# A graph network with an expert layer on one core: the stage behind the second aggregation on a ring, with weights and normalised x split into halves beforehand

## What is computed

```python
x = x + gnn(layernorm(x), edges)          # two graph convolutions
x = x + ffn(layernorm(x))                 # gate over 8 experts, top 1

def gnn(x):                               # 256 -> 512 -> 256
    h = relu(batchnorm(gcn_conv(x, W1)))
    h = batchnorm(gcn_conv(h, W2))
    return relu(h + x)                    # x: the normalised input

def ffn(x):
    H = gelu(x @ W1 + b1)                 # 256 -> 1024
    probs = softmax(H @ Wg + bg)          # 8 experts
    e = argmax(probs)
    return probs[e] * (H @ Wd[e] + bd[e]) # 1024 -> 256
```

## Time and profile before

| | us |
|---|---|
| median of 3 runs | 1978.55 (1978.46 to 1978.88) |
| the profiled execution | 1977.22 |
| its span, first to last instruction | 1975.5 |
| PE busy | 1601.0 (81%) |
| DVE busy | 1182.2 (60%) |
| POOL busy | 993.3 (50%) |
| ACT busy | 884.7 (45%) |
| mean granted TensorE clock | 0.945 of full |

### The profile page before, as it was taken

The page is one execution under the profiler, slowest core; times in us unless marked ns, Lnnn a source line. Parts: engine busy times, 40 slices in busy tenths (PEclk is TensorE's granted clock), DMA queues, the critical chain, the costliest instruction groups (busy, mean ns, idle before and its releaser), DMA issues. The chain is left out here.

```text
span 1975.5 us, 35978 instructions
## 1 busy us (share of the span) xinstructions
PE 1601.0 (81%) x10885; PEld 1227.7 (62%) x10886; DVE 1182.2 (60%) x4427; ACT 884.7 (45%) x1850; POOL 993.3 (50%) x1039
## 2 busy tenths in 40 slices
PE   0010799999999896978999999935589967999997
PEld 0010466666665596965666666613579967999996
DVE  8516788888887666961222122119788884555554
ACT  4126455555554444850010010019678855555553
POOL 5640777777777500017777777701123333555554
PEclk9999999999999988988999999965699988999999
DMA  9953556665665500146666666553330012222221
GB/s 297 281 111 112 175 202 206 221 211 200 206 203 196 183 7 11 56 155 219 224 236 218 221 236 220 187 173 107 110 106 35 32 59 64 71 65 68 70 67 36
DMA packets 157789, 289.15 MB, mean 146 GB/s; under 512 B 39159, under 2 KB 120866, under 8 KB 149835
## 3 DMA queue, kind: packets, MB, share of 16 engines
q1 hardware_dynamic: 104205, 163.76, 24.4%
q0 software_dynamic: 45152, 115.63, 18.9%
q10 hardware_dynamic: 8320, 8.39, 1.4%
HBM read 206.18 MB, written 96.07 MB: 153 GB/s over the span
## 5 line engine op out<-in xcount | busy, mean ns | idle before, releaser
L934 POOL DMA_INDIRECT grows<-table_dram,gsrc x697 | 666.7, 956 | 378.6 <-issue 208.7
L865 PE MATMUL ps<-table,adj 128*128 128x512 f16 x2793 | 695.2, 381 | 12.8 <-DMA adj<-adj_dram 12.8
L865 PEld LDWEIGHTS ps<-table,adj 128*128 128x128 f16 x2793 | 383.0, 142 | 172.6 <-issue 17.5
L894 ACT ACTIVATE adj<-ps 128x490 f16<-128x490 f32 (+1 forms) x390 | 223.5, 573 | 195.1 <-PE ps L800 191.3
L1617 ACT ACTIVATE hf<-ps,b1f 128x256 f32<-128x256 f32 (+1 forms) x424 | 200.9, 475 | 170.6 <-PE ps L1588 167.7
L660 DVE TENSOR_SCALAR oh_r<-iota_r,keyrem 128x128 f16<-128x128 f16 x780 | 212.9, 275 | 42.3 <-PE ps L800 35.8
L661 DVE TENSOR_SCALAR oh_k<-iota_k,keyrem 128x246 f16<-128x246 f16 x780 | 235.7, 307 | 0.0
L1648 DVE SCALAR_TENSOR_TENSOR h_lo<-hf,beta,h_hi 128x256 f16<-128x256 f32 (+1 forms) x424 | 194.7, 481 | 60.5 <-ACT h_hi L1612 55.2
L676 DVE SCALAR_TENSOR_TENSOR tmp_d<-ps,disP,tmp_d 128x256 f32<-128x256 f32 x30 | 14.5, 484 | 326.7 <-ACT tmp_d L900 326.7
L1588 PE MATMUL ps<-xt_hi,fw_hi 128*128 128x256 f32 (+1 forms) x848 | 184.4, 300 | 12.9 <-ACT hf L1617 8.1
L800 PE MATMUL ps<-oh_k,oh_r 128*128 128x245 f16 x780 | 148.7, 273 | 45.6 <-DVE oh_k L661 41.1
(11 more groups left out here) (296 smaller groups left out, 2488.3 us busy)
## 6 DMA issues: line engine op xcount, KB each, us to landing
adj_dram<-adj SPq DMA_DIRECT2D x30, 1568.0 KB
adj<-adj_dram SPq DMA_DIRECT2D x30, 1568.0 KB, 7.3
x_sb<-x SPq DMA_DIRECT2D x12, 1024.0 KB
grows<-table_dram,gsrc POOLq DMA_INDIRECT x697
wd_abs<-fwd ACTq DMA_DIRECT2D x8, 1024.0 KB, 5.7
wd_raw<-fwd SPq DMA_DIRECT2D x8, 1024.0 KB, 5.0
in_rows<-sorted_rows SPq DMA_DIRECT2D x56, 128.5 KB, 2.1
table_dram<-table SPq DMA_DIRECT2D x7, 896.0 KB, 4.0
```

The lines of the kernel that those rows point to most:

```text
L865: last = pe.matmul(acc, adj[:, :, c], table[:, c, :], start=c == 0, stop=c == NT - 1)
L894: act.activation(m.adj[:, q % 3, d0:d0 + wide, :].rearrange("r d c -> r (d c)"), m.ps[:, n % 3, 0:wide * NT], ACT.Copy).then_inc(a.s_adj, 1)
L934: pool.indirect_dma_start(m.grows[:, n % GR, j, :], None, m.table_dram, bass.IndirectOffsetOnAxis(ap=m.gsrc[:, g, part * BT + j:part * BT ...
```

## The change

In the second aggregation a list of 61 items is worked on beside the sums, two per step: 25 pairs of tiles of x are normalised and split into two fp16 halves, 4 pieces of W1 and 32 of Wd are scaled and split likewise. Each is loaded by SP (256 KB), its high half made by ACT and its low half by DVE, and stored by SP to DRAM (256 KB). `finish_gnn` runs on groups of four tiles in a ring of twelve, loads x and the halves of normalised x, adds these on PE by products with the identity and `agg2` by fp32 matmuls with the identity, and lets DVE write x1 straight into `m.rows`, which ACT normalises in place. The FFN's first layer takes fp16 halves, with the scale taken off in the gelu; Wd's halves are loaded by four DMAs in the gate's block. Semaphores of the linear layers are cleared and reused.

```diff
+def convert(m, a, args):
...
+        sp.dma_start(to, from_).then_inc(a.s_raw[n % 2], 16)
...
+    def store(sp, n):
+        what, i = kind(n)
+        sp.wait_ge(a.s_cvlo, n + 1)
...
+        sp.dma_start(to, from_).then_inc(a.s_put[n % 2], 16)
...
+    def high(act, n):
+        what, i = kind(n)
+        act.wait_ge(a.s_raw[n % 2], 16 * (n // 2 + 1))
+        if n >= 2:
+            act.wait_ge(a.s_put[n % 2], 16 * (n // 2))
...
+            for t in range(k):
+                tile = raw(n)[:, t * C:(t + 1) * C]
+                last = act.activation(tile, tile, ACT.Identity, bias=a.xshift[:, 2 * i + t:2 * i + t + 1], scale=m.rstd[:, 2 * i + t:2 * i + t + 1])
+            last.then_inc(a.s_xs, 1)
+            act.wait_ge(a.s_xs, n + 1)
+            act.activation(parts(n)[:, 0:512 * k].rearrange("p (t h c) -> p t h c", h=2, c=C)[:, :, 0, :],
+                           raw(n)[:, 0:C * k].rearrange("p (t c) -> p t c", c=C), ACT.Copy).then_inc(a.s_cvhi, 1)
...
+    def low(dve, n):
+        what, i = kind(n)
+        dve.wait_ge(a.s_cvhi, n + 1)
...
+    def items(k):
+        return range(min(2 * k, NITEM), min(2 * k + 2, NITEM)) if second and k >= 0 else range(0)
...
+                if g in (1, 3):
+                    for n in items(k - 1):
+                        if n % 2 == (g == 3):
+                            cv_low(dve, n)
...
+                if g in (9, 12):
+                    for n in items(k):
+                        if n % 2 == (g == 12):
+                            cv_high(act, n)
...
+        if second:
+            for sem in m.middle:
+                pool.sem_clear(sem)
...
+            for k in range(nd + 3):
+                if k < nd:
+                    if k >= 3:
+                        sp.wait_ge(a.s_dense, blk0 + k - 2)
+                    sp.dma_start(m.adj[:, k % 3, :, :], m.adj_dram[k, :, :, :]).then_inc(a.s_back[k % 3], 16)
+                if k == 0:
+                    cv_load(sp, 0)
+                    cv_load(sp, 1)
+                for n in items(k - 2):
+                    cv_store(sp, n)
+                    if n + 2 < NITEM:
+                        cv_load(sp, n + 2)
+            for q in range(2):
+                sp.wait_ge(a.s_put[q], 16 * len(range(q, NITEM, 2)))
...
+            for q in range(RG):
+                load(q)
...
+            for q in range(len(groups)):
+                sp.wait_ge(s_x1, done[q])
+                store(q)
+                if q + RG < len(groups):
+                    load(q + RG)
+            sp.dma_start(m.w1[:, :, :, :].rearrange("p n h c -> p n (h c)"), m.w1_dram.rearrange("n p f -> p n f")).then_inc(gw.s_w1, 16)
...
+                dve.scalar_tensor_tensor(m.rows[:, t0:t0 + k, 0:C], m.ps[:, g % 4, 0:k * C].rearrange("p (t c) -> p t c", c=C), 0.0,
+                                         xr[:, at:at + k, :], ALU.max, ALU.add).then_inc(s_x1, 1)
...
+            def normalise(q):
+                t0, k = groups[q]
+                act.wait_ge(s_shift3, q + 1)
+                act.wait_ge(s_out[q % RG], 16 * (q // RG + 1))
+                for i in range(t0, t0 + k):
+                    act.activation(m.rows[:, i, 0:C], m.rows[:, i, 0:C], ACT.Identity, bias=shift3[:, i:i + 1], scale=rs3[:, i:i + 1])
+
+            act.wait_ge(s_aff, 1)
+            AHEAD = 4
+            for q in range(AHEAD):
+                affine(q)
+            for q in range(len(groups)):
                 normalise(q)
+                if q + AHEAD < len(groups):
+                    affine(q + AHEAD)
...
+                if t0 % GT == 0:
+                    pe.wait_ge(s_in[q % RG], 32 * (q // RG + 1))
                 if g >= 4:
                     pe.wait_ge(s_x1, g - 3)
+                pe.wait_ge(s_v, q + 1)
                 for i in range(k):
+                    acc = m.ps[:, g % 4, i * C:(i + 1) * C]
+                    for n in range(2):
+                        pe.matmul(acc, m.id16[:, :], xnr[:, (t0 + i) % RT, n * C:(n + 1) * C], start=n == 0, stop=False)
                     for h in range(KC):
-                        last = pe.transpose(m.ps[:, g % 4, i * C + h * P:i * C + (h + 1) * P],
-                                            m.agg2[:, h, (t0 + i) * P:(t0 + i + 1) * P], m.id32[:, :])
-                last.then_inc(s_tr, 1)
-
+                        last = pe.matmul(acc[:, h * P:(h + 1) * P], m.agg2[:, h, (t0 + i) * P:(t0 + i + 1) * P], m.id32[:, :],
+                                         start=False, stop=h == KC - 1)
...
+        half, at = divmod(h * P, 512)
+        for q, (w, x) in enumerate(((0, m.xt_hi), (1, m.xt_hi), (0, m.xt_lo))):
             for k in range(KC):
-                last = pe.matmul(m.ps[:, h % UB, 0:n], w[:, k, h * P:(h + 1) * P], x[:, par, k, 0:n],
+                last = pe.matmul(m.ps[:, h % UB, 0:n], m.w1[:, 2 * k + half, w, at:at + P], x[:, par, k, 0:n],
                                  start=q == 0 and k == 0, stop=q == 2 and k == KC - 1)
...
-            for k in range(1, KH):
-                if k >= 2:
-                    sp.wait_ge(s_wdfree, k - 1)
-                sp.dma_start(wd_raw[k % 2][:, :, :], a.fwd[:, k * P:(k + 1) * P, :].rearrange("e p c -> p e c")).then_inc(s_wd[k % 2], 16)
-            sp.wait_ge(s_wdfree, KH)
+            for e in range(0, NEXP, 2):
+                n = KH // 2
+                sp.dma_start(m.wd[:, e:e + 2, :, :, :, :].rearrange("p e k h t c -> p (e k) (h t c)"),
+                             m.wd_dram[e * n:(e + 2) * n, :, :].rearrange("n p f -> p n f")).then_inc(m.s_wd, 16)
...
-            act.activation(m.w1_hi[:, :, :], w1_raw[:, :, :], ACT.Copy).then_inc(s_w1hi, 1)
...
-                    for k in (2 * n, 2 * n + 1):
-                        act.wait_ge(s_wd[k % 2], 16 * (k // 2 + 1))
-                        act.activation(m.wd_hi[:, :, k, :], wd_raw[k % 2][:, :, :], ACT.Copy, scale=m.alpha[:, k:k + 1]).then_inc(s_wdhi, 1)
...
-            link(dve.tensor_tensor(m.w1_lo[:, :, :], w1_raw[:, :, :], m.w1_hi[:, :, :].bitcast(F32), ALU.subtract))
...
-                if n is not None and n < 4:
-                    for k in (2 * n, 2 * n + 1):
-                        dve.wait_ge(s_wdhi, k + 1)
-                        dve.scalar_tensor_tensor(m.wd_lo[:, :, k, :], wd_raw[k % 2][:, :, :], m.alpha[:, k:k + 1],
-                                                 m.wd_hi[:, :, k, :], ALU.mult, ALU.subtract).then_inc(s_wdfree, 1)
...
+            pe.wait_ge(m.s_wd, 16 * NEXP // 2)
```

More of the change, by code:

```diff
@@ L611, in aggregate_tensors @@
     a.tmp = m.tmp_d
+    a.raw, a.parts, a.xshift = take("cv_raw", [P, 2, 512], F32), take("cv_parts", [P, 2, 1024], F16), a.pick
+    a.s_raw, a.s_put = [m.sem(f"cv_raw{q}") for q in range(2)], [m.sem(f"cv_put{q}") for q in range(2)]
+    a.s_xs, a.s_cvhi, a.s_cvlo, a.s_zero = m.sem("cv_xs"), m.sem("cv_hi"), m.sem("cv_lo"), m.sem("cv_zero")
     S = m.sem
@@ L628, in aggregate @@
+def aggregate(nc, m, args, second, table, agg, dis):
     a = m.agg
@@ L1324, in _ @@
+            sp.dma_start(m.w1[:, :, :, :].rearrange("p n h c -> p n (h c)"), m.w1_dram.rearrange("n p f -> p n f")).then_inc(gw.s_w1, 16)
+            for q in range(RG):
+                sp.wait_ge(s_out[q], 16 * len(range(q, len(groups), RG)))
+            sp.wait_ge(gw.s_w1, 16)
         @block.gpsimd
@@ L1329, in _ @@
             pool.tensor_tensor(rs2[:, :], ve2[:, :], mh[:, :KC], ALU.pow).then_inc(s_rs, 1)
-            for q in range(NT // NG):
-                t = slice(q * NG, (q + 1) * NG)
+            for q, (t0, k) in enumerate(groups):
+                t = slice(t0, t0 + k)
                 pool.wait_ge(s_ve3, q + 1)
@@ L1380, in shifts @@
+                if t0 + k == sum(groups[q]):
+                    first, n = groups[q]
+                    t = slice(first, first + n)
+                    dve.wait_ge(s_sum, first + n)
+                    for i in range(first, first + n):
+                        last = dve.bn_aggr(mv3[:, i, :], st3[:, i, :])
+                    link(last)
+                    dve.tensor_scalar(ve3[:, t], mv3[:, t, 1], XSCALE ** -2, EPS * XSCALE ** -2, ALU.mult, ALU.add).then_inc(s_ve3, 1)
             def shifts(q):
-                t = slice(q * NG, (q + 1) * NG)
+                first, n = groups[q]
@@ L1382, in shifts @@
+                t = slice(first, first + n)
                 dve.wait_ge(s_rs3, q + 1)
                 dve.scalar_tensor_tensor(shift3[:, t], mv3[:, t, 0], -1.0, rs3[:, t], ALU.mult, ALU.mult).then_inc(s_shift3, 1)
-            for g in range(len(pairs) + 2):
+            for g in range(len(pairs) + 1):
                 if g < len(pairs):
-                    add(g)
-                if 1 <= g <= len(pairs):
-                    residual(g - 1)
-                if g >= 2:
-                    stats(g - 2)
@@ L1392, in _ @@
-            dve.wait_ge(s_tr, len(pairs))
-            dve.wait_ge(s_rs3, NT // NG)
-            for i in range(ACTQ * NG, NT):
```

(21 more changed lines are left out.)

265 lines of the change are left out of this document (154 added, 111 removed).

## The result

The changed kernel takes 1923.16 us, median of 4 runs (1922.55 to 1923.37), beside 1978.72 us for the kernel before: a ratio of 0.9718, 95% interval 0.9701 to 0.9735. The forecast was 1926.0, with a range of 1908 to 1958. The profiled execution has a span of 1921.6 us, 53.9 under that of before.

The account below looks back on a forecast made before the run. It took PE to bound the second aggregation and experts, ACT and DVE the stage between, DVE the gate's loop. 1977.2 + 3 - 20.5 - 2 - 19 - 14 = 1924.7, plus 1.3 for the median: 1926.0 us, range 1908 to 1958.

Parts of the forecast that it names:

- Second aggregation: Second aggregation: added item work hidden on ACT and DVE, +2 for the wait on loads and +1 for semaphore clears, +3 us.
- late loads: Second aggregation: 0.9 us of cover in 13 x steps, later landing makes PE wait; +2 us taken, bounds 0 and +26.
- The clears: Second aggregation: 26 semaphore clears on POOL ahead of the first gather, +1 us taken, 0 to 8 possible.
- third rival: Second aggregation: new traffic delays L900 or gathers in all 30 steps, POOL nearly full; 1995 at 2.3 us a step; chance 0.08.
- Stage behind it: Stage behind the second aggregation: clock rises, DMA sets the pace, 71 us for 91.5, -20.5 us; bounds 63 and 80.
- Gate's head: Before the gate's first transpose: L1830, L1856 and their wait go, some 3.3 us left of 5.3; -2 us, bounds 0 and -4.
- First steps of the gate: Gate's first four steps: DVE and ACT lose L1910 and L1841 work, -19 us, bounds -16 and -22.
- Gate's loop: Gate's loop: hidden-layer matmuls go to fp16, but DVE bounds it and its work is unchanged; 0, at best -3 us.
- Experts: Experts' pass, PE-bound: fp16 matmuls cheaper than fp32r, 13.2 us, plus 0.8 from type changes; -14 us, bounds -12 and -18.
- (1): Stage behind the aggregation: PE stays at 1.2 GHz, 5.2 us a group, stage 80 us; total 1936; chance 0.16.
- (2): Second aggregation: x loads land late, 1 to 2 us of PE wait in 13 steps; +20, total 1946; chance 0.17.
- (4): Gate's loop gains as well and the stage behind the aggregation runs at its bytes; total 1912; chance 0.12.

Follow-up runs that it names:

- e1: Changed kernel with low halves of the second aggregation's 61 items written for 8 columns only, loads and stores kept: 1922.96 us, ratio 0.9716.
- e7: Changed kernel with the low half of each x item written in four passes of 128 columns instead of one of 512: 2202.1 us, ratio 0.9819.
- e3: Changed kernel with VectorE's wait for wg and bg and the three instructions behind it moved ahead of the 13th pair: 1921.34 us, ratio 0.9708.
- e4: Changed kernel with Gelu's scale as the constant 2^-21 in place of the operand: 1924.39 us, ratio 0.9722.
- e10: Changed kernel with an extra 0.5 MB DRAM copy queued on SyncE ahead of stores and loads in the 13 x steps: 2229.55 us, ratio 0.9845.
- e11: The changed kernel itself, unedited, run again as base for e12 on the same chip: 1925.8 us, ratio 0.9730.
- e9: Changed kernel with the edits of e3, e5 and e7, and Wd's low halves in passes of 128 columns as well: 2216.9 us, ratio 0.9799.
- e6: Changed kernel with halves of normalised x loaded for the first three groups only, 10 of 13 loads left out: 2176.95 us, ratio 0.9743.
- e8: Changed kernel with the edits of e3, e5 and e7 together: 2193.3 us, ratio 0.9789.
- e12: Same kernel as e8 (changed kernel with the edits of e3, e5 and e7), run beside e11: 1919.4 us, ratio 0.9700.
- e5: Changed kernel with GpSimd's 26 semaphore clears in the second aggregation moved behind its last gather: 2201.0 us, ratio 0.9823.

## Why the prediction was right, step by step

**Second aggregation, +3 forecast, +3.1 measured: right in sum by luck, wrong in its parts.** The loads came as the working had them. In the step that starts at 1019.25 ScalarE ends the second item 13.8 us after the start, the number of the prediction, and TensorE waited for the turn's copy only once in the stage, 1.1 us, as before. So "late loads" cost nothing where +2 was taken. The clears cost 1.7 for the 1 taken. A dense step is 13.6 us in the mean (13.4 before), under the 14 by which the forecast would have fallen, though 7 of 29 are 14.6 us or longer, with shorter ones behind them: TensorE now waits for gathers 5 times, 11.7 us in all, for once and 5.9 before. What the prediction lacks is VectorE's hold on GpSimd: it gave the low halves a duration and called them hidden work, because VectorE had time to spare. They were hidden on VectorE and not on the engine next to it, which had no spare rate, as the prediction itself says in its third rival. The gathers took 6.2 us longer from first to last (e1, e7). Of that and the clears 2.4 came back in TensorE's backlog of batches behind the last gather, and 2.3 at the block's end, for a reason that wasn't found (last section): 1.7 + 6.2 - 2.4 - 2.3 is the 3.1 (rounded). Without these 2.3, which no term of the forecast had, it would have been 5.4. In this stage the trace of before could not show the hold: there every gather takes 1.01 us or less, and VectorE has no pass with two full operands in SBUF (its one-hots compare one tensor with a column, the pass at a step's end reads PSUM). In the first aggregation it could. One gather of 374 takes 1.21 us, the others 1.04 at most, and it lies over L687, which adds one SBUF tensor to another:

```profile
214.68 1.21 POOL L934 DMA_INDIRECT grows<-table_dram,gsrc  x1 [0.30 <-issue]
```

```profile
214.72 0.74 DVE L687 TENSOR_TENSOR adj<-adj,id 128x128 f16<-128x128 f16 x1
```

One such row of 374 is easily missed, and most of the 30 passes of L687 cost a gather nothing.

The Trainium skill ("SBUF — State Buffer", SBUF: two separate sides) states that VectorE and GpSimd share a pair of ports as an exclusive lock: whichever starts first gets the pair for the whole instruction, and the other is blocked. For a pass with two SBUF inputs it states this only against a GpSimd operation that reads SBUF. A gather reads its row numbers (`gsrc`) from SBUF; that this read is what waits was not tested. The traces agree with the rule: every gather that starts in a pass of the changed kernel ends 0.82 us after the pass does, one that starts ahead of it isn't lengthened, e1 has no long gather once the passes are short, and e7 a shorter hold for a shorter pass. That only some of the passes cost anything (24 passes of 0.69 us lengthen at most 18 of the first 170 gathers in any profile with whole passes) is a matter of where in the 1.25 us from gather to gather a pass falls.

**Stage behind it, -20.5 forecast, -23.5 measured.** The mechanism is the one forecast: the clock rose (0.96 in the window), TensorE isn't the bound, DMA is. Two terms of the sum were mis-sized, in opposite directions. The group was taken at 4.7 us, from the 349 GB/s of loads alone; the ring's mix of loads and stores ran at 374 to 383 GB/s, 4.1 to 4.2 us, and the first three groups were there already when the first residual was written. From the first residual to the end of the last it took 48.3 us for the 57.6 of the sum. The start was taken at 6.5 us and took 13.9: the wait of L1509, which the working passed over although the diff puts a wait for the last two loads of the queue ahead of VectorE's first residual. The prediction had listed the new waits of this stage, SyncE's and ScalarE's, and not this one. e3 prices it at 3 to 3.7 us. The tail, 6.5 taken, is 5.9.

**Gate's head, -2:** right; 3.3 us from the stage's end to the first transpose, as written.

**First steps of the gate, -19 forecast, -20.2 measured.** Right: without Wd's halves the steps are 6.6 to 6.8 us where they were 10.6 (and 15.3 for the one that took the last two), and ScalarE is busy for 27.7 of 31 us.

**Gate's loop, 0:** right, 15.46 us for two steps before and after. The reason given holds: VectorE's work is unchanged. But one change was not costed at all, Gelu's scale operand, 88 ns on each of ScalarE's instructions. It cost nothing because ScalarE had that much room; at 100.2 of 110 us little is left. The Trainium skill ("ScalarE: Activation LUTs", What ACT_TABLE_LOAD costs) puts each such operand at about 93 ns; e4's 88 ns agree.

**Experts, -14 forecast, -13.3 measured.** Right in place and size. One step of the chain that ended last, changed kernel, beside the earlier trace rows:

```profile
1860.31 1.31 PE ps L1755 x12
1861.62 0.44 PE ps L1741 x4
1862.06 3.93 PE ps L1755 x36
1865.99 5.24 PE ps L2167 x48
```

10.92 us a step for 11.43; 36 fp16 products in 3.93 us are 0.1092 each, the 0.1096 of the forecast. The first 12 and the transposes take 1.75 us for 1.87, and that is the 12 products at 0.1092 for 0.1192 each; the four transposes take 0.44 us in both. So the "0.8 of changes of type" isn't there: the 13.2 for the products alone is next to the 13.3 measured.

**The rivals.** (1), TensorE at half clock: that clock lasted from the first product at 1315.1 to 1320.5, and came back from 1331.0 to 1334.3, after TensorE had waited 4.9 us for the ring; otherwise it was full. The price of TensorE's work was right: at half clock its instructions start 0.213 us apart, six to a tile, 1.28 us for the 1.29 reckoned, and at full clock 0.111 us apart, 2.7 us a group for 3.0. (The eight instructions of L1477 are not eight pairs, and each has 128 columns of weights and one that moves; their 0.213 us between starts fitted all the same.) (2), loads late: not in the changed kernel; e10, meant to force it, could not. (3), every step delayed: its mechanism, GpSimd without spare rate, is real, its price 0.2 us a step and not 1.8. (4), the loop gains too: no (15.47 us for two steps before and after); the other half of it, the stage near its bytes, is what happened.

## What to carry to other kernels

Work that fills an engine's idle time is hidden only if it is hidden from the engines beside it too: here VectorE passes with both operands in SBUF cost time to a GpSimd that issues gathers back to back, and short passes cost it less. Where an engine's instructions are now and then longer than their median, look at what its neighbour had just begun. When a load is moved to the end of a queue, look for the wait on it that stands ahead of other work, here one wait in front of the first residual for 3 us. And where the engine that issues the pacing instructions is full from end to end, everything put in front of its first one delays them all, here by 1.7 us; what the stage then pays of it no run shows by itself.

## What the runs showed of the hardware

- A gather's issue on GpSimd, 0.95 us alone, takes up to 1.46 us (e11) when it starts in a VectorE pass of 0.69 us with both inputs in SBUF: it ends 0.82 us after the pass does. Beside passes of 128 columns (0.29 us for x, 0.35 for Wd, e9) it takes 1.11 us at most; e9's longest, 1.15 us, is beside a pass of W1, which kept its 512 columns. Beside the one-hots of the second aggregation before the change it takes 1.01 us at most.
- Clearing a semaphore on GpSimd costs 65 ns.
- From the end of the last transposes of the aggregation to the next stage's first load it takes 2.0 us in the changed kernel and in e1 to e6, e9 to e11, and 4.3 to 4.5 us in the kernel before, e7, e8 and e12, with the same work in between. VectorE is the last to arrive: from its last branch in the aggregation to its next instruction, a drain, the traces record 2.8 us in e12, 2.9 before and 0.5 in the changed kernel. It goes with the program, not with the run (e8 and e12 are one kernel, on two chips). What in the program decides it wasn't found; it is worth 2.3 us, beside the 6.4 that e12 gains.
- In e5 to e10 TensorE's dense steps took 16 us at a granted clock of 0.91 to 0.93 (e5, e7, e9, e10, 1050 to 1500 us; 13.4 us at 1.00 in the changed kernel), with the records of its products no longer than usual. There the edits in the aggregation bring nothing, and the comparisons with the kernel before were 0.974 to 0.985 where they are 0.970 to 0.974 in the other runs. What it hangs on is open: the record gives e5 to e8 chip 1 and e9 and e10 chip 5, and chip 5 is also that of e1 to e4, which kept 13.4 us.
